# Layer norm's rows turned in the opening stage, output weights in four loads, and a zero fill one stage earlier

## The reference

```python
x = x + tanh(g_xattn[0]) * L0_xattn(layernorm(x), ctx_512)   # causal attention over 56 keys
x = x + tanh(g_ffn[0])   * L0_ffn(layernorm(x))              # softmax, top 8 of 64
x = x + tanh(g_xattn[1]) * L1_xattn(layernorm(x), ctx_512)   # latent attention, 1500 keys
x = x + tanh(g_ffn[1])   * L1_ffn(layernorm(x))              # ternary weights, Hadamard
x = x + tanh(g_xattn[2]) * L2_xattn(layernorm(x), ctx_512)   # latent attention, rope on the queries
x = x + tanh(g_ffn[2])   * L2_ffn(layernorm(x))
x = x + tanh(g_xattn[3]) * L3_xattn(layernorm(x), ctx_512)   # as L0
x = x + tanh(g_ffn[3])   * L3_ffn(layernorm(x))              # 8 experts, 1 per row, and a shared one
# layer norm: (x - mean) / sqrt(var + eps) over 256 features; x is 16 x 56 rows of 256
```

## Time and profile before

| | |
|---|---|
| median of 3 runs | 1586.06 us (1582.59 to 1588.73) |
| profiled execution, its own time | 1583.63 us |
| its span, first to last instruction | 1581.8 us |
| mean granted clock of TensorE | 0.982 of full |
| PE busy | 1493.4 us, 94% |
| DVE, ACT, POOL busy | 885.9, 666.4, 644.6 us |

### The profile page before, as it was taken

One profiled execution on the slowest core, in us unless ns is written; L12 is line 12 of the kernel. 1 busy time (PEld: TensorE's weight loads), 2 busy tenths in 40 slices (PEclk: granted clock), 3 DMA queues, 4 the chain that ended last, 5 costly groups with the idle time before them and its releaser, 6 DMA issues. The chain is left out here.

```text
span 1581.8 us, 39572 instructions
## 1 busy us (share of the span) xinstructions
PE 1493.4 (94%) x17140; PEld 1208.6 (76%) x17152; DVE 885.9 (56%) x1596; ACT 666.4 (42%) x971; POOL 644.6 (41%) x458
## 2 busy tenths in 40 slices
PE   6899899999999999879998999999999999888998
PEld 3585788888888877666656888888888878855466
DVE  5853656565656527875556556565656253477112
ACT  4534444445444433542013444544454424255221
POOL 1208665456544100734966644654462007222101
PEclk9999999999999999999997999999999999999999
DMA  8045654655454113224035646444632021062402
GB/s 245 2 108 118 134 131 108 140 123 126 111 133 96 42 53 74 89 76 103 6 74 118 140 114 142 102 107 111 142 70 64 2 93 32 1 255 63 168 21 67
DMA packets 66461, 154.47 MB, mean 98 GB/s; under 512 B 14972, under 2 KB 44220, under 8 KB 65424
## 3 DMA queue, kind: packets, MB, share of 16 engines
q1 hardware_dynamic: 65520, 150.10, 37.8%
q0 software_dynamic: 768, 1.84, 0.4%
HBM read 87.51 MB, written 5.51 MB: 59 GB/s over the span
## 5 line engine op out<-in xcount | busy, mean ns | idle before, releaser
L1820 DVE TENSOR_REDUCE latent_psW<-latent_psW 128x1 f32<-128x500 f32 x630 | 403.8, 683 | 218.9 <-PE latent_psW L1716 218.2
L1799 ACT ACTIVATE latent_w<-latent_psS 125x896 f32<-125x896 f32 x384 | 351.8, 919 | 410.9 <-PE latent_psS L1734 407.4
L1744 PEld LDWEIGHTS latent_psO<-latent_val,latent_w 125*64 125x64 f32 x10752 | 323.9, 138 | 25.9 <-issue 12.4
L1744 PE MATMUL latent_psO<-latent_val,latent_w 125*64 125x65 f32 x10752 | 339.7, 223 | 1.1 <-issue 1.1
L1733 PE MATMUL latent_psS<-latent_qA,latent_kA 128*125 128x448 f32 x768 | 289.6, 377 | 6.0 <-DVE latent_qB L1837 2.4
L1734 PE MATMUL latent_psS<-latent_qB,latent_kB 128*125 128x448 f32 x768 | 281.9, 367 | 0.0
L1716 PE MATMUL latent_psW<-latent_kA,latent_qA 128*128 128x500 f32 x642 | 208.4, 395 | 1.2 <-DVE latent_mx L1824 1.2
L1733 PEld LDWEIGHTS latent_psS<-latent_qA,latent_kA 128*125 128x125 f32 x768 | 142.9, 186 | 31.4 <-ACT latent_w L1799 4.6
L1734 PEld LDWEIGHTS latent_psS<-latent_qB,latent_kB 128*125 128x125 f32 x768 | 143.0, 186 | 22.0 <-issue 2.2
L1716 PEld LDWEIGHTS latent_psW<-latent_kA,latent_qA 128*128 128x128 f32 x642 | 122.1, 191 | 14.7 <-DVE latent_mx L1824 3.3
L1071 POOL TENSOR_TENSOR latent_rawT<-latent_rawT,latent_ropeT 128x1000 f32<-128x1000 f32 x48 | 110.6, 2330 | 41.5 <-DVE all_xn L279 33.6
(11 more groups left out here) (434 smaller groups left out, 2169.9 us busy)
## 6 DMA issues: line engine op xcount, KB each, us to landing
latent_qA<-latent_qh SPq DMA_DIRECT2D x128, 112.0 KB, 2.4
latent_rawT<-in_ctx_cols SPq DMA_DIRECT2D x32, 375.0 KB, 5.5
latent_rawT<-in_ctx_cols SPq DMA_DIRECT2D x64, 187.5 KB, 5.9
latent_raw<-in_ctx SPq DMA_DIRECT2D x32, 375.0 KB
latent_kA<-latent_high SPq DMA_DIRECT2D x32, 375.0 KB, 4.0
latent_kB<-latent_high SPq DMA_DIRECT2D x32, 375.0 KB, 5.9
latent_kA<-latent_rawT SPq DMA_DIRECT2D x32, 375.0 KB, 5.4
experts_wgu<-in_L_gu SPq DMA_DIRECT2D x8, 1024.0 KB, 15.0
```

Of the source, the lines that this page charges most:

```text
L1744: last = pe.matmul(sums[r:r + 64, c, :], w[t % ROUND][:, queries_of(c, r):queries_of(c, r) + 64], val[b % 2][:, t, :], start=(t == 0 and c ...
L1799: act.activation(w[t % ROUND][:, :].rearrange("p (h n) -> p h n", h=2), psS[0:KP, t % 2, :, 0:GH], ACT.Exp).then_inc(exp_done, 1)
L1820: dve.tensor_reduce(bank[:, THIRD + j:THIRD + j + 1], bank[:, 0:THIRD], mybir.AxisListType.X, ALU.max).then_inc(max_ready, 1)
```

## The change

Four things. (1) `begin` now does layer 0's norm: moments, root, scaled rows and turned tiles in four groups of two, with 4, 4, 1, 1, 1, 1, 1, 1 unread products ahead of the tiles, and PE waits for the identity alone. The first attention has lost its norm. `Tanh` of the gates is in the first attention, on ACT after the queries, and the first `add` on DVE waits for it. POOL clears `values` at the start of that stage, as layer 3 did. (2) `queries_roped` loads `wo` in four parts with a semaphore each, and PE waits for `wkv` and the part it needs, DVE for the rope table. (3) The zeros of `sorted_x` are stored in layer 3's attention, from a small tile `none`, in 14 transfers behind the loads of that stage. (4) In `experts_ffn` PE turns tile 0 ahead of the last shared unit and ACT copies it there; the wait for the last shared result now stands in `gate_up` of tiles 0 and 1.

```diff
@@ -371,9 +371,13 @@
         stats_done = a.sem("stats_done")
-        done = a.sem("done")
-        raw = a.sb("gates_raw", [128, 8])
+        eps_ready = a.sem("eps_ready")
+        raw = g.gates_raw
+        ident_came = a.sem("ident_came")
         ps = a.ps("ps", [128, 512])
+        norm = Norm(nc, a, g)
+        norm.GROUPS = tuple((2 * p, 2 * p + 2) for p in range(NT // 2))
+        PAIRS = NT // 2
         with nc.Block() as block:
@@ -382,29 +386,40 @@
                     if p == 0:
-                        sp.dma_start(g.ident[:, :], d["ident"]).then_inc(came, 16)
+                        sp.dma_start(g.ident[:, :], d["ident"]).then_inc(ident_came, 16)
                 sp.dma_start(raw[:, 0:4], d["g_xattn"].partition_broadcast(128)).then_inc(came, 16)
...
                 ahead.wait(sp)
-                sp.wait_ge(came, 48)
+                sp.wait_ge(came, 32)
...
             def _(pe):
-                pe.wait_ge(came, 48)
-                keep_busy(pe, g, ps[:, 0:128], 8)
+                pe.wait_ge(ident_came, 16)
+                for t in range(NT):
+                    keep_busy(pe, g, ps[:, 0:128], 4 if t < 2 else 1)
+                    norm.tensor_tile(pe, t)
...
             def _(dve):
-                dve.memset(g.eps[:, :], EPS)
+                dve.memset(g.eps[:, :], EPS).then_inc(eps_ready, 1)
                 ahead.pad(dve)
-                for t in range(NT):
-                    take_moments(dve, g, t, x_came[t // 2], 16, stats_done)
+                for p in range(PAIRS + 1):
+                    if p < PAIRS:
+                        for t in range(2 * p, 2 * p + 2):
+                            take_moments(dve, g, t, x_came[p], 16, stats_done).then_inc(norm.mv_ready, 1)
+                    if p >= 1:
+                        norm.vector_group(dve, p - 1)
...
             def _(act):
-                act.wait_ge(came, 48)
-                act.activation(g.gates[:, :], raw[:, :], ACT.Tanh).then_inc(done, 1)
+                act.wait_ge(eps_ready, 1)
+                for p in range(PAIRS + 1):
+                    if p < PAIRS:
+                        norm.root_group(act, p)
+                    if p >= 1:
+                        norm.scalar_tile(act, 2 * p - 2)
+                        norm.scalar_tile(act, 2 * p - 1)
@@ -504,23 +519,26 @@
                     loads(sp)
+                if router:
+                    sp.wait_ge(ahead.emptied, 1)
+                    for j in range(SLOT_TILES):
+                        sp.dma_start(ahead.sorted_x[j * 128:(j + 1) * 128, :], ahead.none[:, :]).then_inc(ahead.zero_stored, 16)
                 ahead.wait(sp)
                 later.wait(sp)
+                if router:
+                    sp.wait_ge(ahead.zero_stored, 16 * SLOT_TILES)
...
             def _(pool):
-                if layer:
-                    pool.memset(values[:, :, :, :, :], 0.0).then_inc(emptied, 1)
+                pool.memset(values[:, :, :, :, :], 0.0).then_inc(emptied, 1)
                 pool.memset(qT[:, :, T:T + 8], 0.0).then_inc(zeroed, 1)
...
                 later.clear(pool)
-                if not layer:
-                    pool.wait_ge(taken, 2 + QQ)
-                    pool.memset(values[:, :, :, :, :], 0.0).then_inc(emptied, 1)
-
+                if router:
+                    pool.memset(ahead.none[:, :], 0.0).then_inc(ahead.emptied, 1)
                 for p in range(NP):
@@ -529,18 +547,12 @@
             def _(pe):
-                def turn_rows():
-                    norm.tensor(pe)
-                    pe.wait_ge(norm.xnT_ready, NT)
-
                 weights.wait(pe)
...
                               ctxT[:, 8 * h:8 * h + 8, 0, :], start=True, stop=True).then_inc(prod, 1)
-                if not layer:
-                    turn_rows()
                 for n in range(QQ):
@@ -652,15 +664,13 @@
-                if not layer:
-                    norm.root(act)
                 take_keys()
-                if not layer:
-                    norm.scalar_tiles(act)
                 for n in range(QQ):
...
                     act.mul(qT[:, m, h * HALF:(h + 1) * HALF], ps_a[:, n % 2, 0:HALF], HD ** -0.5).then_inc(taken, 1)
+                if opening:
+                    act.activation(g.gates[:, :], g.gates_raw[:, :], ACT.Tanh).then_inc(gates_ready, 1)
@@ -713,8 +723,6 @@
             def _(dve):
-                if not layer:
-                    norm.vector(dve)
                 step = Chain(dve, chain)
@@ -749,6 +757,8 @@
                     dve.wait_ge(y_done, p + 1)
+                    if opening and p == 0:
+                        dve.wait_ge(gates_ready, 1)
                     dve.scalar_tensor_tensor(out=g.x[:, p, :], in0=ps_y[0:TP, 0:C], scalar=gate, in1=g.x[:, p, :],
@@ -1388,7 +1398,9 @@
         rope = a.sb("rope", [128, 4, 3, S])
-        came_o = a.sem("came_o")
+        came_kv, came_rope = a.sem("came_kv"), a.sem("came_rope")
+        PARTS = 4
+        came_o = [a.sem(f"came_o{n}") for n in range(PARTS)]
         G = a.sb("G", [128, CC, 2, NH * LO], F32R)
@@ -1416,9 +1428,11 @@
             def _(sp):
-                sp.dma_start(wkv[:, :, :], d["L2_wkv"].rearrange("k (h n) -> k h n", h=NH)).then_inc(came_o, 16)
-                sp.dma_start(wo[:, :, :], d["L2_wo"].rearrange("k (h n) -> k h n", h=NH)).then_inc(came_o, 16)
-                sp.dma_start(rope[:, :, :, :], d["rope_q"]).then_inc(came_o, 16)
+                sp.dma_start(wkv[:, :, :], d["L2_wkv"].rearrange("k (h n) -> k h n", h=NH)).then_inc(came_kv, 16)
+                for n in range(PARTS):
+                    some = slice(n * NH // PARTS, (n + 1) * NH // PARTS)
+                    sp.dma_start(wo[:, some, :], d["L2_wo"].rearrange("k (h n) -> k h n", h=NH)[:, some, :]).then_inc(came_o[n], 16)
+                sp.dma_start(rope[:, :, :, :], d["rope_q"]).then_inc(came_rope, 16)
                 sp.wait_ge(g_done, NH)
@@ -1434,7 +1448,9 @@
                     if h == OUTS:
-                        pe.wait_ge(came_o, 48)
+                        pe.wait_ge(came_kv, 16)
+                    if h >= OUTS and (h - OUTS) % (HP // PARTS) == 0:
+                        pe.wait_ge(came_o[(h - OUTS) // (HP // PARTS)], 16)
                     if h >= OUTS:
@@ -1522,7 +1538,7 @@
                     norm.low_tile(dve, t)
-                dve.wait_ge(came_o, 48)
+                dve.wait_ge(came_rope, 16)
                 for n in range(NU):
@@ -2615,8 +2634,6 @@
             def _(sp):
-                sp.wait_ge(cleared, 2)
-                sp.dma_start(tiled(sorted_x), rows[:, :, :]).then_inc(zero_stored, 16)
                 for e in range(NE):
@@ -2637,8 +2654,6 @@
                 pool.memset(ones[:, :], 1.0).then_inc(cleared, 1)
-                pool.memset(rows[:, :, :], 0.0).then_inc(cleared, 1)
-                pool.wait_ge(zero_stored, 16)
                 pool.wait_ge(xs_ready, NT)
@@ -2668,7 +2683,7 @@
                 pe.matmul(ps_d[0:TP, 1, NT * NE:(NT + 1) * NE], ones[:, :], cum[:, NT, :], start=True, stop=True).then_inc(places_done, 1)
-                for n in range(1, UNITS):
+                for n in range(1, UNITS - 1):
                     shared_unit(n)
@@ -2684,6 +2699,8 @@
                         pe.wait_ge(inner_ready, j - 1)
+                    else:
+                        pe.wait_ge(h_ready, UNITS - 1 + j)
                     for off, ps, done in ((0, ps_g, gate_done), (F3, ps_u, up_done)):
@@ -2708,10 +2725,10 @@
+                turn(0)
+                shared_unit(UNITS - 1)
                 pe.wait_ge(slots_ready, 2)
                 pe.wait_ge(g.wgu_came, 16 * NE)
-                pe.wait_ge(h_ready, UNITS)
-                turn(0)
                 experts = []
@@ -2739,7 +2756,15 @@
                 act.activation(sg[:, :], top[:, :], ACT.Sigmoid).then_inc(sg_ready, 1)
+                def take_turned(j):
+                    act.wait_ge(turned, j + 1)
+                    if j >= 2:
+                        act.wait_ge(up_done, j - 1)
+                    act.copy(xT[:, j % 2, :, :], ps_t[:, 0, 0:CC * 128].rearrange("p (c n) -> p c n", c=CC)).then_inc(xT_ready, 1)
+
                 for n in range(UNITS):
+                    if n == UNITS - 1:
+                        take_turned(0)
                     act.wait_ge(g_done, n + 1)
@@ -2750,19 +2775,12 @@
-                def take_turned(j):
-                    act.wait_ge(turned, j + 1)
-                    if j >= 2:
-                        act.wait_ge(up_done, j - 1)
-                    act.copy(xT[:, j % 2, :, :], ps_t[:, 0, 0:CC * 128].rearrange("p (c n) -> p c n", c=CC)).then_inc(xT_ready, 1)
-
                 def take_inner(j):
-                take_turned(0)
                 for j in range(SLOT_TILES + 1):
@@ -2871,6 +2889,7 @@
         g.gates = a.sb("gates", [128, 8])
+        g.gates_raw = a.sb("gates_raw", [128, 8])
         g.eps = a.sb("eps", [128, 1])
```

13 lines of the change are left out of this document (8 added, 5 removed).

## The result

The changed kernel takes 1567.55 us (median of 4, 1566.74 to 1569.65) against 1586.26 of the kernel before (4, 1582.59 to 1588.73): a ratio of 0.9886, 95% interval 0.9864 to 0.9908. The profiled execution took 1568.31, 15.3 less than that of before.

A forecast was written before the change was run, and what follows sets the result against it. PE, busy 94% of 1581.8 us, bounds the kernel; gains lie where it waits or runs slow. -3.0 - 5.9 - 2.1 = -11.0 from the profiled 1583.6 gives 1572.6, 1575.0 for a median; range 1569.5 to 1581.

The forecast's parts named there:

- part 1: The opening, begin and layer 0's attention up to the first scores: 3.0 us less, bounds 1.6 and 5.4.
- the growth of the begin: Begin gets longer by the turned tiles of layer 0's norm: 2.8 us more, from 2.0 to 3.7.
- the saving in the attention: Layer 0's attention without its norm, from stage start to first scores: 12.3 for 18.1, 5.8 us saved, bounds 5.3 and 7.4.
- part 3: Last stage, zeros stored earlier and tile 0 ahead of the last shared unit: expert loop 2.1 us sooner, bounds 1.1 and 2.3.
- shifted, not changed: The rest of the program, untouched by the edits, was taken to move in time only, its loads issued on moving events.
- the slow end: Layer 0's attention to first scores takes 12.8 us, as layer 3's copy without a norm and with slow key products.
- The fast end: Layer 0's attention to first scores takes 10.7 us; held out of reach if ACT's key masking delays the second query product.
- Part 2: Layer 2's queries, output weights in four loads: wait of 2.94 and slow clock of 3.0 go, 5.9 us less.
- The new wait for the rows: PE at tile 0 waits for the sorted rows, the last shared unit queued behind: 1.2 us if they land at 1476.5.
- no quarter was late: Rival at layer 2's queries: the weight quarter lands after 709.83, PE still waits, its clock falls; 1579.4, chance 0.13.
- PE did not stay at its lower clock: Rival: spread unread products leave PE at its lower level into layer 0's attention loop, 21 us more, 1596; chance 0.04.
- The opening's rival: Begin's turning stays at the lower clock, attention starts at 17 or later, the opening gives 0; 1578.0, chance 0.13.

The follow-up runs named there:

- the zeros alone: The kernel before with the zeros of the sorted rows stored a stage sooner and nothing else: median 1584.45 us, ratio 0.9994.
- the zeros late: The kernel before with tile 0 turned ahead of the last shared unit and zeros stored as before: 1596.88 us, one profile.

## Why the prediction was wrong

All stages below are read over 18 profiles of 16 kernels, each grouped by whether it has the part in question.

```
                                          before's way           changed               by stage  I had
first key product                         13.41-14.57 (7)        14.62-15.85 (8)       +1.3      +2.8
key product to first scores               16.7-18.6 (7)          11.33-11.56 (8)       -6.4      -5.8
queries: first product to last output     23.1-25.2 (6)          17.9-19.0 (10)        -5.5      -5.9
slots to first expert product             21.82-21.85 (5)        19.10-19.16 (11)      -2.75     -2.1
```

Left out are, in each line, the kernels that change a piece of that stage; only the one with the values cleared late is kept in the first two, where its clearing comes behind the first scores.

Two steps of the prediction failed. The first are two terms of part 1, the growth of the begin, put at 2.8 and measured at 1.3, and the saving in the attention, put at 5.8 and measured at 6.4; a smaller one is in part 3. The second is that the rest is "shifted, not changed", which left too narrow a range for what executions of unchanged code differ by.

**Part 1** is where the miss is: -3.0 on record, -5.1 to the first scores (31.74 to 26.68, means), -7.7 by times. Two terms were mis-sized. The growth of the begin was 2.8 and measured 1.3: I took a value between DVE's path and a cold PE, which came out right for the profiled pair (13.41 to 15.85 is +2.4); but the trace of before happened to be the earliest of seven with its opening, whose mean is 14.01. And I took 12.3 from the stage's start to the scores, nearer the slow end because ACT's masking might hold up the second query product. It did, by 0.54, and yet the stretch is 11.34 from the first key product nearly every time (11.56 in one), for PE had its upper clock throughout. The fast end was the right row to lean on: layer 3's copy loses 2.1 in its key products, which the new opening does not. The old opening, on the other hand, lost more than the records showed me: PE stops for the turned tiles and runs part of its queries at the lower clock, which the earlier trace rows hold in the 7.97. From the profile of before:

```profile
19.81 0.63 PE L321 MATMUL xattn_ps_b<-all_ident,all_xn 112*128 112x112 f32 x4 [2.35 <-ACT all_xnT L298]
```

```profile
22.00:24.00 2.00, 1.57 (x5) 0.88 (x4) 1.23 (x2) 0.59 (x2) 0.00 (x0) 0.68 1.08 246
24.00:27.00 3.00, 3.00 (x6) 1.38 (x5) 0.00 (x0) 0.54 (x1) 0.00 (x0) 0.64 1.14 257
```

The first exponential now comes about 4.2 behind the first scores and not 5.4 to 5.7, with the values cleared and no table load just ahead of it. Yet nothing was won by either, as I had it, for the last fold does not come sooner. From the first scores to the last fold it is 47.8 to 48.2 in either opening, and 48.7 to 49.7 where a stretch at the lower clock falls there: 3 of 7 before, 2 of 8 with the change. The 2.6 between the 5.1 of the stage and the 7.7 of the times has no place that I can show. The interval of the times (6.6 to 8.7) excludes 5.1, so its cause stays open; the times of the zeros alone are off by 1.9 in the same way.

**Part 2** went as forecast. The wait of 2.94 is gone, the lower clock behind it too, each shown by itself: with the wait kept and PE at work through it, the stretch behind output product 0 is 2.9 shorter; with one load the wait is there (2.73). In the profiled pair the stage is 6.0 shorter. Over all profiles it is 5.5, since of the six profiles with the common wait three have a shorter stretch at the lower clock behind it (3.4, and the stage takes 23.1) and three a longer one (6.8, 25.0 to 25.2); that of before is one of the longer. Times put it at 3.9, 2.8 to 5.0: a little too much was forecast from the one execution that I had. The rule of the Trainium skill that I weighed against it (DMA: Bandwidth & Descriptors, Bandwidth: batch to 1 MiB or more) decides nothing here. Estimated by its figures, which are for transfers that GpSimd issues, a quarter would have taken 1.5 to 3.8 behind `wkv`. These are issued by SP, and in the ten profiles with the split the first quarter landed 1.2 to 1.6 behind `wkv`, where I had 1.2. In the profile after, the four loads of 512 KB land 5.5 to 7.8 after their issue; one of 2 MB takes 8.3 to 9.2 in the eight profiles that have it, and no product waits for a quarter.

**Part 3** was mis-sized by 0.7. The scatter starts 1.65 sooner by the slots (I had 2.4, and within 0.3 of them; it is 1.07, and what POOL does until then I can't show), and that is worth nothing alone. What I left out is that the gain is a removed chain: with the unit ahead of both tiles, as the rows of the zeros alone show, PE waits 0.99, 0.61 and 0.61 for the last `hT` and for two copied tiles, and these 2.2 vanish when the unit lies between the turned tiles; each tile then costs 0.22 and not 0.4, the unit 3.01 and not 3.1. 0.22 + 3.01 + 0.22 is 3.45, where I summed 3.9. The new wait for the rows hardly came: they were read 3.1 ahead of tile 0 and take 2.8; the weight load ahead of tile 0 waited 0.33 for them, and tile 0 started 15.65 after the slots, where the last unit used to. With the zeros late it comes at once, 4.41 long. The two halves of part 3 are one change.

**The sum.** -11.0 on record; -13.4 by stages; -14.5 by the times of the parts; -15.5 as a whole; -18.7 in the four executions shown. Of the 7.7 that the forecast lacks, 2.1 are part 1's stage and 0.7 part 3's, with 0.4 too much in part 2; 2.1 lie between the stages and the whole and stay open; and 3.2 are the four executions, which were quicker than the thirteen later ones. That last piece is luck as far as I can tell, and without it the time, 1570.4, would have come out inside the range, with part 1 mis-sized all the same.

The second step that failed is the sentence that the rest is "shifted, not changed". The instructions are, the time is not: from the last fold of layer 0's attention to the first query product of layer 2 it took 620.5 to 626.5, and from the last output product to the slots 729.7 to 736.8 in the six kernels without the earlier zeros, with nothing edited in either. My range had 2.8 and 0.5 beyond its bounds for this; the means of two samples of the changed kernel differ by 3.8. None of the rivals came: no quarter was late, the opening gave its full share and more, and PE did not stay at its lower clock. The opening's rival had the right mechanism, though: without the unread products or with a stop for the gates, PE enters the attention cold and gives back 0.6 to 2.3.

## What to carry to other kernels

Size a moved stage from the row that has the same clock as the new one will have, and ask for each edit whether it keeps the tensor engine at work up to the next stage: here the stop for two gates cost 2.3, of which the table load and `Tanh` were 1.5. A wait is worth its length and the slow stretch that may follow it; the two can be measured apart by unread products through the wait. Where one wait stands for several loads, look at when each of them landed: here the last 2.0 of 2.94 were for a table that PE did not need. Two edits that meet at one wait are one change: here, in their stage, the one alone gave 0 and the other alone lost 3.6. And when whole executions of unchanged code spread by 17 us, a part of 3 us is read in its own stage over several profiles, never from one pair.

## What the runs showed of the hardware that I had not expected

In the 18 profiles the granted clock falls to 0.50 for 3.4 to 20.5 us at a time. Some places are the same in all of them (near 160, 685, 830, 1375 and 1445), others come in some executions alone (between 615 and 640 in eight of the 18), and the length differs from one execution to the next. Such stretches add up to 35 to 80 us in executions of one and the same kernel, which are 1578.2 to 1595.5 long.

Standing still is not enough to make it fall, and the length of the stop does not decide it. Before output product 0 PE stood for 2.94 in the profile of before, and for 2.38, 2.55, 3.38, 3.57 and 4.26 in the five others in which it waits there for all three loads; the lower clock followed each time. With one load and its own wait it stood for 2.73, longer than two of these, and the granted clock stayed at 1.00. That is one profile; what decides stays open.

An interval can leave out no change and still mislead in size: the mean of the zeros alone lies 1.9 below the kernel before (95% 0.1 to 3.6, over all executions of it; the ratio 0.9994 with its interval, 0.9976 to 1.0012, does not leave out no change), while from the slots to the first expert product it takes 21.85 in both.
